# A graph network on one core: products of ones in TensorE's waits at the first ranks and at the head of places 0, 1 and 2

## The chip, the cores and the metric

The kernel runs on one core of a Trainium2 chip. The metric is device time of one execution in microseconds, lower is better. The engines: TensorE (PE: matmuls; PEld: its weight loads), VectorE (DVE), ScalarE (ACT), GpSimd (POOL) and SyncE (SP, which here only issues DMAs). Each runs its own instruction stream in order and waits on semaphores.

## The reference

`x` is 3125 x 256 (fp32), `src` and `dst` hold 50,000 edges, sorted by `dst`. Four layers of a graph network follow on a layer norm:

```python
def sage(x, src, dst, Wl, Wr, b):
    agg = segment_sum(x[src], dst, n)
    deg = segment_sum(ones_like(dst), dst, n)
    return (agg / maximum(deg, 1)[:, None]) @ Wl + x @ Wr + b

h = maximum(layernorm(x), 0)
h = relu(sage(h, ..1)); h = relu(sage(h, ..2)); h = relu(sage(h, ..3))
out = x + sage(h, ..4)
```

## The kernel before

**Counts.** The kernel turns the edge list into a dense matrix `counts` (source node by destination node, fp16, kept in SBUF), so that a layer's sum over edges is a matmul of `H` (the features, split in a high and a low fp16 part) with `counts`. Destinations are cut in 7 chunks of 512 (the last has 53); a chunk at its turn is a *place*, q = 0 to 6, and `ORDER` says which chunk: 5, 6, 4, 3, 2, 1, 0. The counts of a pair of *windows* of 16 destinations in all are made by `step`: VectorE writes one-hot columns for a few edges at a time ("hot" columns, L1460 and L1467), TensorE multiplies them into a PSUM bank (L2091), and ScalarE copies the bank into `counts` (L1817, semaphore `window_stored`).

**Ranks.** Before that, each window's first edge has to be found. The edges lie in 98 rows of 512. `sum_below` (L1969) multiplies 16 times 0/1 comparisons (made by VectorE, L1179, L1182 and, for the low windows, `below_low`, L1230) with a block of ones and so counts edges below each bound: the first rank has 72 columns (into `degree_ps`), the second 108 (`turn_bank`), the third, `rank_low`, 512. ScalarE takes each rank out of PSUM (L1895, semaphore `lo_made`). VectorE then chooses rows (`choose_early`, L1238 and L1250, semaphore `steps_chosen`), and TensorE selects them (`select_rows`, L1978). In between VectorE and ScalarE do the layer norm of chunk after chunk (`h0_moments`, `h0_shift`, `h0_relu`, ...), TensorE its transposes (`h0_turn`, L2036) and the products with `Wr1` (`own_products`, L2048).

**Order of the work.** It is written out by hand, engine by engine: tables such as `between`, `first_round` and `second_round` say what is done after which window or which source tile k. TensorE's stream (from L1966 on): the two first ranks, the two selections, 32 window pairs for place 0 with `select_edges`, `h0_turn`, `own_products` and `rank_low` among them, then `heavy_of(-1)`, then the loop over the places. For each place it adds up 25 source tiles (`add_sources`, L2262; first half "sum", other half "half") while it makes the window pairs of the next place and finishes the place before (`lin_part`, L2156; `narrow_part`, L2205). Degrees come from differences of neighbouring hot cuts (`sum_cuts`, L2297, then `take_degrees` on VectorE, L1541), but in place 1 (`BY_COUNTS`) from the counts themselves (`add_degrees`, L2279: 25 products of two columns, then `degrees` on VectorE, L1605 and L1607). `heavy_of(q)` ends a place's windows: it waits until they are stored, looks in registers for windows with more edges than the planned steps, and branches over them; it does this after place q for q = -1, 0, 1 and on. The beginning of a place on TensorE:

```python
heavy_of(-1)
for q in range(NCH):
    pe.wait_ge(window_stored, filled_after(q - 1))
    if q == BY_COUNTS:
        add_degrees(q)           # waits for own_copied, 2 * IN_LIN
    elif q < NCH - 1:
        sum_cuts(q)              # waits for cuts_made; in place 0 for lo_made, 3
    if q > BY_COUNTS:
        pe.wait_ge(low_done[1], q - 1)
    ...
        if k == 0 and q >= 1:
            pe.wait_ge(agg_scaled[1], 2 * q - 1)
        add_sources(1, q, 0, k, k == 0, k == NT - 1, halves=(0,))
```

The wait on `agg_scaled` is for VectorE's `scale_agg` (L1559), which empties the PSUM bank of the place before. On VectorE's stream the first instruction is a memset of the tail tile of `x` (L1160), for which SP's load of that tile waits; it goes on with the edge rows once their DMA has landed (L1172). After layer 1 come layers 2 to 4, which only sum, multiply and turn; the change touches nothing there.

Of the kernel before, what the change touches and what calls it, by code (L numbers as in the profile page):

```python
# [26 lines left out]
def sage_stack_kernel(nc, x, src, dst, Wl1, Wr1, b1, Wl2, Wr2, b2, Wl3, Wr3, b3, Wl4, Wr4, b4, out):  # L27
# [10 lines left out]
    f32, f16, bf16, i32 = mybir.dt.float32, mybir.dt.float16, mybir.dt.bfloat16, mybir.dt.int32  # L38
    ALU, ACT, AX = mybir.AluOpType, mybir.ActivationFunctionType, mybir.AxisListType

    P = 128
# [6 lines left out]
    CH = TPC * P  # L48
# [37 lines left out]
    for w_, (d0_, _) in enumerate(WINDOWS):  # L86
        PAIR_WINDOWS[d0_ // (2 * WIN)].append(w_)
# [80 lines left out]
    for at_, (w, i) in enumerate(STEP):  # L168
        if i:
            continue  # L170
        k = STEPS[w]
# [8 lines left out]
    BY_COUNTS = 1  # L180
# [75 lines left out]
    def filled_after(q):  # L256

        return sum(len(FILLS[p]) for p in range(-1, q + 1))
# [15 lines left out]
    with ctx:  # L274
        def sb(name, shape, dt):
            return ctx.enter_context(nc.sbuf_tensor(name, shape, dt))

        def pb(name, shape, dt):
            return ctx.enter_context(nc.psum_tensor(name, shape, dt))

        def sem(name):
            return ctx.enter_context(nc.semaphore(name))
# [44 lines left out]
            return at[:, 0:n * P], at[:, n * P:n * (P + KEYS)]  # L327
        WR2 = 2 * 2 * F2
        Wr2_sb = early[:, 0:WR2].bitcast(f32).rearrange("p (k n) -> p k n", k=2)
        cut_at = sb("cut_at", [P, WIN + 2], bf16)  # L330
        minus_one = sb("minus_one", [P, 2], f16)
        plan_all = sb("plan", [P, 2 * NWIN], i32)
# [155 lines left out]
        window_ps = pb("window_ps", [P, 2, 512], f32)  # L488
        degree_ps = pb("degree_ps", [P, 512], f32)
        agg_ps = pb("agg_ps", [P, 2, 512], f32)  # L490
        lin_ps = pb("lin_ps", [P, 2, 512], f32)
        turn_bank = pb("turn_ps", [P, 512], f32)
# [10 lines left out]
        act_order = sem("act_order")  # L503
        pool_order = sem("pool_order")
        pads_set = sem("pads_set")
        consts_made = sem("consts_made")
        dst_loaded = sem("dst_loaded")
        src_loaded = sem("src_loaded")
# [53 lines left out]
        own_copied = sem("own_copied")  # L562
# [130 lines left out]
        IN_LIN = 5  # L693
        FIRST_J = 3
        LAST_DEGREE_TURN_K = 22
        BY_STEPS_IN_AGG = 2
# [442 lines left out]
        def load_heavy(eng, regs, part):  # L1139
            chunks = slice(ORDER[2], NCH) if part == 0 else slice(0, ORDER[2])  # L1140
            eng.wait_ge(plan_made, 3 * part + 3)
            eng.load(regs[1][chunks], heavy[0:1, chunks])
# [13 lines left out]
        def _(dve):  # L1156
            order = Order(dve, dve_order)
            v = nc.vector

            v.memset(x_in[NFULL][:, 0, :], 0.0).then_inc(tail_cleared, 1)  # L1160

            def row_starts(n):
# [804 lines left out]
        def _(pe):  # L1967
            m = nc.tensor.matmul
            def sum_below(below, ps, n, at=0):  # L1969
                for g in range(RG):  # L1970
                    last = m(ps[:, 0:n], ones16[0:RP, :], below[g][:, at:at + n], start=(g == 0), stop=(g == RG - 1))
                last.then_inc(rank_summed, 1)
# [31 lines left out]
            def select_edges():  # L2004
# [6 lines left out]
                                 start=True, stop=True)  # L2011
                last.then_inc(steps_turned, 1)

            pe.wait_ge(consts_made, CONSTS_RANK)
            pe.wait_ge(below_made, 1)
            sum_below([below_high[0:RP, g, :] for g in range(RG)], degree_ps, BOUNDS - CUT)
            pe.wait_ge(below_made, 2)
            sum_below([below_mid[0:RP, g, :] for g in range(RG)], turn_bank, CUT - MID)
            pe.wait_ge(rows_shifted, 2)
            pe.wait_ge(steps_chosen, 1)  # L2020
            select_rows(0, [chosen_first[0:RP, g, :] for g in range(RG)], FIRST)
# [128 lines left out]
            def lin_part(q, j):  # L2150

                n, t = size_of(chunk_at(q))
                if j == 0:
                    pe.wait_ge(agg_scaled[1], 2 * (q + 1))
                h, k = j // 2, j % 2
                last = m(lin_ps[:, h, 0:n], W14[:, 0, k, h * P:(h + 1) * P], aggT[:, k, 0:n], start=(k == 0),  # L2156
                         stop=(k == 1))
                if k == 1:
                    last.then_inc(lin_done[1], 1)
# [110 lines left out]
            def add_degrees(q):  # L2270

                c = chunk_at(q)
                n, t = size_of(c)
                rows_ = P if n == CH else n
                pe.wait_ge(own_copied, 2 * IN_LIN)
                for i in range(t):
                    for k in range(NT):
                        of = slice(0, TAIL if k == NT - 1 else P)
                        last = m(lin_ps[0:rows_, 0, 2 * i:2 * i + 2], counts[of, k, bass.ds((c * TPC + i) * P, rows_)],  # L2279
                                 ones16[of, 0:2], start=(k == 0), stop=(k == NT - 1))  # L2280
                last.then_inc(degree_done, 1)
# [58 lines left out]
            heavy_of(-1)  # L2340
            for q in range(NCH):

                pe.wait_ge(window_stored, filled_after(q - 1))
                if q == BY_COUNTS:
                    add_degrees(q)
                elif q < NCH - 1:
                    sum_cuts(q)
                if q > BY_COUNTS:
                    pe.wait_ge(low_done[1], q - 1)
                for kind, k in script(q):  # L2350
                    if kind == "step":
                        step(*k)
                    if kind == "half":
                        if k == 0 and q >= 1:
                            pe.wait_ge(agg_scaled[1], 2 * q)
                        add_sources(1, q, 0, k, k == 0, k == NT - 1, halves=(1,))
                    if kind == "lin":
                        lin_part(q - 1, k)
                    if kind == "narrow":
                        narrow_part(q - 1, k)  # L2360
                    if kind != "sum":
                        continue
                    if k == 1 and q == BY_COUNTS:
                        pe.wait_ge(degree_inverted, q + 1)
                    if k == CUT_SUM_K and q == NCH - 1:
                        sum_cuts(q)
                    if q == 0 and k in LOW_AT:
                        pe.wait_ge(h0_low, LOW_AT[k])
                    if q == 0 and k in first_round:
                        first_round[k]()  # L2370
                    if q == 1 and k == H0_LATE_K:
                        pe.wait_ge(degrees_taken, 1)
                        pe.wait_ge(norms_made, 3)
                        for j in range(IN_LIN, NCH):
                            h0_turn(j)
                    if q == 1 and k in OWN_LATE_K:
                        own_products(IN_LIN + OWN_LATE_K.index(k))
                    if q == 1 and k == TURN_K:
                        pe.wait_ge(own_copied, 2 * NCH)
                    if k == 0 and q >= 1:  # L2380
                        pe.wait_ge(agg_scaled[1], 2 * q - 1)
                    add_sources(1, q, 0, k, k == 0, k == NT - 1, halves=(0,))
                    if q == BY_COUNTS and k == LAST_DEGREE_TURN_K:
                        turn_degrees(q)
                    if q >= 1 and k == TURN_K:
                        turn(1, q - 1, 0)
                if q == 1:
                    load_heavy(pe, regs, 1)
                    pe.wait_ge(step_tables, 5)
                heavy_of(q)  # L2390
# [100 lines left out]
```

## Time and profile before

| | us |
|---|---|
| median of 3 runs | 659.92 (659.35 to 660.34) |
| the profiled execution, its own time | 660.46 |
| its span, first to last instruction | 658.6 |
| TensorE busy / VectorE / ScalarE / GpSimd | 616.8 / 277.9 / 177.8 / 42.0 |
| mean granted TensorE clock | 0.984 |

The rows below are of one execution; their times count from its first instruction. "Granted clock" is the share of TensorE's full clock (2.4 GHz) that it had in a stretch, 1.00 or 0.50 (1.2 GHz). A row of a timeline merges neighbouring instructions of one group: start, time from the first one's start to the last one's end, engine, line, operands, and how many; in brackets how long the engine stood idle before it and whom it waited for. A matmul's end includes the way through the array, so two rows that follow each other overlap a little. In the chain of waits each line is a piece of the path that ended last; "issue" is time in which nothing that the profile shows was waited for.

### The profile page before, as it was taken

The numbers are of one execution on the slowest core, as the hardware profiler recorded it, in microseconds if no ns is written. First come the engines' busy times: TensorE is split into PE (matmuls) and PEld (weight loads), VectorE is DVE, ScalarE is ACT, GpSimd is POOL, SyncE is SP. The second block draws the span as 40 slices with busy tenths as digits, with TensorE's granted clock in tenths as the row PEclk, the third lists the DMA queues.
The fourth block names the chain that finished last, engine by engine and source line by source line (L and its number), as shares of the span: only waits on it lengthen the run. The fifth ranks groups of instructions, "written<-read, shape, count | busy, mean of one in ns | idle before, by whom it ended". The sixth has DMA issues, their size and how long they took to land.

```text
span 658.6 us, 9693 instructions
## 1 busy us (share of the span) xinstructions
PE 616.8 (94%) x3861; PEld 338.7 (51%) x3862; DVE 277.9 (42%) x529; ACT 177.8 (27%) x379; POOL 42.0 (6%) x93
## 2 busy tenths in 40 slices
PE   5668999798999999998999999999999999999998
PEld 4434565455555445553444445444445555646686
DVE  5979877678888769811212121211120100101011
ACT  3877853364653622300111011121110000000000
POOL 8002100000000000000000000000001011010110
PEclk9977998999999999999999999999999999999999
DMA  8400510520221132241533621344430223032030
GB/s 259 101 0 15 97 33 2 179 56 21 69 34 53 33 53 65 49 136 48 160 88 110 130 81 49 101 119 140 117 121 1 60 65 111 1 111 85 28 112 32
DMA packets 64872, 51.48 MB, mean 78 GB/s; under 512 B 36600, under 2 KB 49437, under 8 KB 64828
## 3 DMA queue, kind: packets, MB, share of 16 engines
q1 hardware_dynamic: 64472, 50.27, 27.3%
q0 software_dynamic: 240, 0.37, 0.7%
q8 instruction: 30, 0.49, 0.4%
q10 hardware_dynamic: 116, 0.24, 0.1%
q14 instruction: 14, 0.11, 0.1%
HBM read 28.68 MB, written 16.60 MB: 69 GB/s over the span
## 4 chain that ended last, share of the span: by engine, by line
PE 78%; DMA 7%; DVE 7%; ACT 3%; issue 2%; SPq 1%; POOL 1%; DVEq 0%; ACTq 0%; POOLq 0%
PE agg_ps L2262 28%; PE window_ps L2262 18%; PE lin_ps L2180 6%; PE lin_ps L2197 5%; PE window_ps L2091 4%; PE lin_ps L2156 3%; DMA rdeg_d<-newH 2%; PE lin_ps L2048 2%; PE window_ps L2238 2%; PE agg_ps L2238 2%; DVE early L1467 1%; DMA rdeg_d<-rdeg 1%; PE lin_ps L2205 1%; ACT counts L1817 1%; DMA newH<-rdeg_d 1%
## 5 line engine op out<-in xcount | busy, mean ns | idle before, releaser
L2262 PE MATMUL agg_ps<-counts,H 128*128 128x512 f16 (+3 forms) x1026 | 235.0, 355 | 2.8 <-DVE aggT L1559 2.5
L2262 PEld LDWEIGHTS agg_ps<-counts,H 128*128 128x128 f16 (+1 forms) x1026 | 79.4, 99 | 58.5 <-issue 12.3
L1817 ACT ACTIVATE counts<-window_ps 128x400 f16<-128x400 f32 x150 | 73.5, 506 | 64.0 <-PE window_ps L2091 50.0
L1460 DVE TENSOR_TENSOR counts<-early 128x2048 f16<-128x2048 bf16 x66 | 77.4, 1214 | 6.2 <-PE window_ps L2091 4.3
L2262 PE MATMUL window_ps<-counts,early 128*128 128x512 f16 (+2 forms) x346 | 77.6, 379 | 0.0
L2262 PE MATMUL window_ps<-counts,H 128*128 128x512 f16 (+2 forms) x291 | 55.3, 346 | 0.0
L2262 PEld LDWEIGHTS window_ps<-counts,early 128*128 128x128 f16 (+1 forms) x346 | 33.6, 98 | 41.5 <-issue 3.4
L1559 DVE SCALAR_TENSOR_TENSOR aggT<-agg_ps,columns,rdeg 128x512 f32<-128x512 f32 (+1 forms) x27 | 17.0, 658 | 80.2 <-PE agg_ps L2262 63.6
L2091 PEld LDWEIGHTS window_ps<-counts 128*128 128x128 f16 x412 | 30.9, 99 | 37.0 <-issue 4.9
L1460 DVE TENSOR_TENSOR early<-early 128x1024 f16<-128x1024 bf16 (+1 forms) x69 | 43.8, 684 | 6.5 <-PE window_ps L2091 4.9
L2262 PE MATMUL agg_ps<-counts,early 128*128 (+4 forms) x297 | 46.5, 314 | 0.0
L2091 PE MATMUL window_ps<-counts 128*128 128x100 f16 x412 | 41.6, 210 | 4.3 <-DVE counts L1460 2.4
L2091 PE MATMUL window_ps<-early 128*128 128x100 f16 (+1 forms) x256 | 32.9, 228 | 9.8 <-DVE early L1467 8.1
L2091 PEld LDWEIGHTS window_ps<-early 128*128 128x128 f16 x256 | 21.3, 101 | 36.6 <-issue 8.1
L2262 PEld LDWEIGHTS window_ps<-counts,H 128*128 128x128 f16 x291 | 24.9, 98 | 29.2 <-issue 1.5
L1122 POOL TENSOR_TENSOR newH<-newH,plan 128x256 f32<-128x256 f32 (+1 forms) x25 | 17.3, 723 | 345.0 <-DMA newH<-in_x_dram 345.0
L1862 ACT ACTIVATE newT<-newT,columns 128x512 f32<-128x512 f32 (+1 forms) x21 | 13.4, 663 | 91.4 <-DVE newT L1695 65.8
L1559 DVE SCALAR_TENSOR_TENSOR aggT<-window_ps,columns,rdeg 128x512 f32<-128x512 f32 (+1 forms) x13 | 9.0, 712 | 67.1 <-PE window_ps L2262 64.3
L1580 DVE SCALAR_TENSOR_TENSOR partsT<-newT,columns,partsT 128x512 f16<-128x512 f32 (+1 forms) x16 | 10.6, 662 | 57.7 <-ACT partsT L1876 57.6
L2262 PEld LDWEIGHTS agg_ps<-counts,early 128*128 128x128 f16 (+1 forms) x297 | 22.0, 97 | 24.3 <-issue 1.1
L1681 DVE TENSOR_TENSOR newT<-lin_ps,newH 128x512 f32<-128x512 f32 (+1 forms) x11 | 7.3, 666 | 50.6 <-PE lin_ps L2180 50.6
L1862 ACT ACTIVATE newT<-lin_ps,columns 128x512 f32<-128x512 f32 (+1 forms) x14 | 8.9, 633 | 69.2 <-PE lin_ps L2197 69.2
(246 smaller groups left out, 636.3 us busy)
## 6 DMA issues: line engine op xcount, KB each, us to landing
selfT<-hT_d SPq DMA_DIRECT2D x18, 512.0 KB, 4.1
rdeg<-rdeg_d SPq DMA_DIRECT2D x24, 256.0 KB, 4.5
hT_d<-newT SPq DMA_DIRECT2D x12, 512.0 KB, 4.4
counts<-in_x_dram SPq DMA_DIRECT2D x6, 512.0 KB, 8.0
hT_d<-counts SPq DMA_DIRECT2D x6, 512.0 KB, 3.4
newH<-in_x_dram SPq DMA_DIRECT2D x6, 512.0 KB
out_dram<-newT SPq DMA_DIRECT2D x5, 512.0 KB
hT_d<-newT SPq DMA_DIRECT2D x6, 256.0 KB, 3.8
```

Source lines behind the costliest of these rows:

```text
L1122: nc.gpsimd.tensor_tensor(x4[0:q, i, :], x4[0:q, i, :], b4rows[0:q, :], ALU.add).then_inc(x4_biased, 1)
L1460: v.tensor_tensor(hots_of(group).rearrange("p r a (n d) -> p r a n d", d=2), pairs.unsqueeze(1).unsqueeze(1).broadcast_to([P, n, 2, P // 2 ...
L1559: v.scalar_tensor_tensor(out=aggT[:, h, 0:n], in0=(agg_ps, window_ps)[bank][:, h, 0:n], scalar=unscale[:, l - 1:l], in1=rdeg[:, 0:n], op0= ...
L1817: a.activation(counts[:, :, 2 * w * WIN:2 * (w + 1) * WIN].rearrange("p t (a w) -> p a t w", a=2), window_bank(FILL_AT[w])[:, 0:2 * KEYS]. ...
L1862: a.activation(newT[:, h, 0:n], source, ACT.Relu, bias=bT[:, bias + h:bias + h + 1]).then_inc(relu_done[l], 1)
L2048: last = m(h0_ps(j)[h][:, 0:n], W14[:, 1, k, h * P:(h + 1) * P], x_T[c][:, k, 0:n], start=(k == 0), stop=(k == 1))
L2091: m(window_bank(at)[:, key0:key0 + keys], one_src, one_key, start=(j == 0), stop=(j == STEPS[w] - 1)).then_inc(hot_used, 1)
L2156: last = m(lin_ps[:, h, 0:n], W14[:, 0, k, h * P:(h + 1) * P], aggT[:, k, 0:n], start=(k == 0), stop=(k == 1))
L2180: last = m(lin_ps[0:rows_, g, i * D:(i + 1) * D], h, w, start=(j == 0), stop=(j == len(ops) - 1))
L2197: last = m(lin_ps[:, h, 0:n], w, r, start=(i == 0), stop=(i == len(ops) - 1))
L2238: last = m((agg_ps, window_ps)[bank][:, h, cols], tile[:, part, h * P:(h + 1) * P], counts[0:rows_, k, c * CH + g * HALF_CH:c * CH + (g + ...
L2262: last = m((agg_ps, window_ps)[bank][:, h, 0:n], tile[:, part, h * P:(h + 1) * P], counts[0:rows_, k, chunk_cols(c, n)], start=first and p ...
```

## The change

Twenty-five products are added to TensorE's stream by a new helper, `keep_clock(ps, times)`. Each multiplies one column of ones, repeated to 128 x 128, with the same column repeated to 128 x 512, and writes a PSUM bank that holds nothing wanted at that moment; the next use of the bank overwrites it, and nobody reads the products. The ones are a new tile of two columns, set by a memset that is now VectorE's first instruction. There are eleven products at the very start, before the wait for the first rank's input; two between the second rank and the first selection; four at the head of place 0; four at the head of place 1, after a wait on `own_copied` that `add_degrees` had, and has, too; four in place 2 before the wait on `agg_scaled`.

```diff
@@ -327,6 +327,7 @@
             return at[:, 0:n * P], at[:, n * P:n * (P + KEYS)]
         WR2 = 2 * 2 * F2
         Wr2_sb = early[:, 0:WR2].bitcast(f32).rearrange("p (k n) -> p k n", k=2)
+        one = sb("one", [P, 2], f16)
         cut_at = sb("cut_at", [P, WIN + 2], bf16)
         minus_one = sb("minus_one", [P, 2], f16)
         plan_all = sb("plan", [P, 2 * NWIN], i32)
@@ -503,6 +504,7 @@
         act_order = sem("act_order")
         pool_order = sem("pool_order")
         pads_set = sem("pads_set")
+        one_set = sem("one_set")
         consts_made = sem("consts_made")
         dst_loaded = sem("dst_loaded")
         src_loaded = sem("src_loaded")
@@ -1157,6 +1159,7 @@
             order = Order(dve, dve_order)
             v = nc.vector

+            v.memset(one[:, :], 1.0).then_inc(one_set, 1)
             v.memset(x_in[NFULL][:, 0, :], 0.0).then_inc(tail_cleared, 1)

             def row_starts(n):
@@ -2011,11 +2014,19 @@
                                  start=True, stop=True)
                 last.then_inc(steps_turned, 1)

+            def keep_clock(ps, times):
+
+                for _ in range(times):
+                    m(ps, one[:, 0:1].broadcast_to([P, P]), one[:, 0:1].broadcast_to([P, CH]), start=True, stop=True)
+
+            pe.wait_ge(one_set, 1)
+            keep_clock(window_ps[:, 0, :], 11)
             pe.wait_ge(consts_made, CONSTS_RANK)
             pe.wait_ge(below_made, 1)
             sum_below([below_high[0:RP, g, :] for g in range(RG)], degree_ps, BOUNDS - CUT)
             pe.wait_ge(below_made, 2)
             sum_below([below_mid[0:RP, g, :] for g in range(RG)], turn_bank, CUT - MID)
+            keep_clock(window_ps[:, 0, :], 2)
             pe.wait_ge(rows_shifted, 2)
             pe.wait_ge(steps_chosen, 1)
             select_rows(0, [chosen_first[0:RP, g, :] for g in range(RG)], FIRST)
@@ -2340,6 +2351,11 @@
             heavy_of(-1)
             for q in range(NCH):

+                if q == 0:
+                    keep_clock(turn_bank[:, :], 4)
+                if q == BY_COUNTS:
+                    pe.wait_ge(own_copied, 2 * IN_LIN)
+                    keep_clock(lin_ps[:, 0, :], 4)
                 pe.wait_ge(window_stored, filled_after(q - 1))
                 if q == BY_COUNTS:
                     add_degrees(q)
@@ -2377,6 +2393,8 @@
                         own_products(IN_LIN + OWN_LATE_K.index(k))
                     if q == 1 and k == TURN_K:
                         pe.wait_ge(own_copied, 2 * NCH)
+                    if k == 0 and q == BY_STEPS_IN_AGG:
+                        keep_clock(lin_ps[:, 0, :], 4)
                     if k == 0 and q >= 1:
                         pe.wait_ge(agg_scaled[1], 2 * q - 1)
                     add_sources(1, q, 0, k, k == 0, k == NT - 1, halves=(0,))
```

## Rows read from the trace of the kernel before

**Rows 1.** Page of the kernel before: engine totals, and granted clock in 40 slices
```profile
PE 616.8 (94%) x3861; PEld 338.7 (51%) x3862; DVE 277.9 (42%) x529; ACT 177.8 (27%) x379; POOL 42.0 (6%) x93
...
PEclk9977998999999999999999999999999999999999
```

**Rows 2.** Stretches: from:to, length, busy us (instructions) by engine, clock, DMA, GB/s
```profile
27.42:37.66 10.24, 7.17 (x36) 3.42 (x35) 9.93 (x31) 9.31 (x23) 0.00 (x0) 1.00 0.03 7
37.66:44.49 6.83, 4.91 (x16) 2.23 (x17) 6.52 (x29) 6.61 (x22) 0.00 (x0) 0.50 0.00 1
44.49:51.32 6.83, 4.37 (x29) 2.55 (x27) 3.05 (x14) 4.26 (x14) 0.00 (x0) 1.00 0.01 4
51.32:58.14 6.82, 5.02 (x20) 2.21 (x19) 6.43 (x25) 4.01 (x13) 0.00 (x0) 0.50 0.07 9
...
105.93:109.34 3.41, 3.41 (x21) 3.35 (x21) 2.55 (x8) 1.18 (x4) 0.00 (x0) 0.50 0.03 6
...
129.82:133.24 3.42, 3.42 (x21) 1.82 (x19) 1.69 (x2) 1.51 (x3) 0.00 (x0) 0.50 0.37 112
```

**Rows 3.** Timeline of TensorE, 5 to 16: start, length, line, operands, count [idle before]
```profile
6.32 1.12 PE L1971 MATMUL degree_ps<-counts,newH 98*128 98x72 f16 x16 [6.32 <-POOL early L1038]
7.29 1.62 PE L1971 MATMUL turn_ps<-counts,newH 98*128 98x108 f16 x16
9.01 1.86 PE L1978 MATMUL agg_ps<-counts 98*128 98x64 f16 x32
10.97 3.28 PE L1978 MATMUL lin_ps<-counts 98*128 98x115 f16 x32
```

**Rows 4.** Timeline of VectorE, 4.9 to 11
```profile
5.00 0.30 DVE L1172 TENSOR_SCALAR counts<-H 98x32 f16<-98x32 int32 x1 [3.86 <-DMA H<-in_dst_dram]
...
6.09 1.14 DVE L1182 TENSOR_TENSOR counts<-counts 98x1728 f16<-98x1728 f16 x1
7.83 0.31 DVE L1238 TENSOR_TENSOR counts<-counts 98x64 f16<-98x64 f16 x1 [0.59 <-ACT counts L1895]
...
9.34 0.16 DVE L1238 TENSOR_TENSOR counts<-counts 98x7 f16<-98x7 f16 x1 [0.48 <-issue]
```

**Rows 5.** Timeline of all engines from the start: ScalarE takes the two ranks
```profile
7.47 0.32 ACT L1895 ACTIVATE counts<-degree_ps,counts 128x72 f16<-128x72 f32 x1 [0.91 <-PE degree_ps L1971]
...
8.95 0.35 ACT L1895 ACTIVATE counts<-turn_ps,counts 128x108 f16<-128x108 f32 x1 [1.15 <-PE turn_ps L1971]
```

**Rows 6.** Timeline of TensorE, 40.5 to 47: the rank of the low windows
```profile
41.02 5.32 PE L1971 MATMUL degree_ps<-counts,newH 98*128 98x512 f16 x16 [1.31 <-DVE counts L1230]
```

**Rows 7.** Chain that ended last, 44 to 56: start, length, what
```profile
47.54 1.98 ACT counts L1817 x5
49.52 0.58 ACT counts L1895
```

**Rows 8.** Timeline of TensorE, 47 to 54: where place 0 begins
```profile
50.50 0.40 PE L2297 MATMUL degree_ps<-aggT,newH 128*128 128x512 f16 x1 [2.17 <-ACT counts L1895]
```

**Rows 9.** Chain that ended last, 100 to 110: where place 1 begins
```profile
103.70 0.61 issue
104.31 0.94 PE lin_ps L2279 x25
...
105.75 1.84 PE window_ps L2036 x8
```

**Rows 10.** Timeline of TensorE, 126 to 140: where place 2 begins
```profile
129.12 0.59 PE L2262 MATMUL agg_ps<-counts,H 128*128 128x512 f16 x2 [1.73 <-DVE aggT L1559]
...
130.81 1.05 PE L2262 MATMUL agg_ps<-counts,H 128*128 128x512 f16 x2
...
131.99 1.05 PE L2262 MATMUL agg_ps<-counts,H 128*128 128x512 f16 x2
...
135.28 0.59 PE L2262 MATMUL agg_ps<-counts,H 128*128 128x512 f16 x2
...
135.89 0.59 PE L2262 MATMUL agg_ps<-counts,H 128*128 128x512 f16 x2
```

## The prediction

> **What bounds the kernel now.** I began with the page's shares and its slices [rows 1]: TensorE is busy for 616.8 us, 94% of the span, so an edit pays only where TensorE runs slowly or where another engine waits for it. The clock line is below 9 in three slices only, all in the first fifth. The second view cuts the span where the granted clock changes [rows 2]. It is at 0.50, the 1.2 GHz level, in four stretches: 37.66 to 44.49, 51.32 to 58.14, 105.93 to 109.34 and 129.82 to 133.24; the reader is to see TensorE busy all the time in the last two (3.41 of 3.41, 3.42 of 3.42), while in the second VectorE is just as full (6.43 of 6.82). Third, TensorE's timeline at the start [rows 3]. The profile shows a clock of 1.00 there, but the durations say otherwise: 16 products of 72 columns in 1.12 us and 32 of 115 columns in 3.28 us are some 1.2 columns a nanosecond, the lower level. So the ranks run at half rate too, though no row of the clock says it.
>
> Who waits for those ranks is in VectorE's timeline [rows 4] and in ScalarE's two rows [rows 5]: TensorE sums a rank, ScalarE takes it out of PSUM (0.32 and 0.35), VectorE chooses rows with it. VectorE stands still for 0.59 before 7.83 and 0.48 before 9.34. Last come the chains of waits where places 0 and 1 begin [rows 7, 9] and TensorE's timeline where places 0 and 2 begin [rows 8, 10].
>
> **The change part by part.** Price of one product of 512 columns: the rank of the low windows has 16 of them in 5.32 us from 41.02 [rows 6]; the first 3.47 us of that lie before 44.49, at half rate. 3.47/(2b) + 1.85/b = 16 gives b = 0.22 at full rate and 0.45 at half. No row has a product whose two operands are both one repeated column. Below, 0.22 stands; above, 0.45, as if it always went at half rate. I take 0.22, since every other 512-column product goes at what the clock gives.
>
> *The memset of ones* lies in VectorE's idle 3.86 us before 5.00 [rows 4]: nothing. The memset behind it, for which SP's load of the tail of x waits, comes later by less than that memset's own length; nothing again.
>
> *Eleven products before the first rank.* TensorE does nothing until 6.32 [rows 3]. They start at about 1.0 and at half rate take 11 x 0.45 = 4.9, so they end by 5.9 and delay nothing. If they lift the clock, the second rank, which starts at 7.29 when its input is made (6.09 + 1.14 [rows 4]), is shorter: 16 x 108 columns go from about 1.6 to 0.9. VectorE's second choice moves from 9.34 to 8.64, 0.70 earlier; the first, which the end of 6.09 + 1.14 also holds, moves by 0.44 and no longer decides. From there VectorE is nearly full until 41 (9.93 of 10.24 from 27.42 on [rows 2]), so the 0.70 arrives at the low rank. There half is lost: if the clock still rises at 44.49, that rank only starts 0.70 earlier into the low stretch, and 0.70 at half rate is worth 0.35. I take -0.35; bounds 0 (no lift) and -0.70.
>
> A reason to doubt the lift: TensorE is busy almost without a pause from 6.32 to 14.25 [rows 3], and the clock stays low. The difference that I see is in size: stretches that ended with a rise held 512-column products [rows 6, 10] or fp32 transposes [rows 9], while those before 14.25 have 64 to 115 columns. The eleven have 512, so I take the lift. The Trainium skill, page "TensorE: Matmul & The Clock Gate", section "What's actually happening", says that the clock is throttled by default and that activity releases it. The trace agrees at 44.49, and disagrees from 6.32 to 14.25. By that rule the start gains what I took, and by the row nothing; the sum is then 658.1 or 658.5.
>
> *Two products between the second rank and the selection.* 0.44 at full rate, 0.9 at half. The selection waits for VectorE's first choice anyway, and its result is wanted only once VectorE is through the second choice and the first statistics, past 12: nothing. At half rate too the cover is over 1 us.
>
> *Four products at place 0.* They stand behind heavy_of(-1), which waits for the last window store (1.98 from 47.54, so 49.52 [rows 7]). So they do not fill the wait of 2.17 us [rows 8]; they follow most of it. In place 1 TensorE takes 0.61 from the store to its first product [rows 9]; taken here, it arrives at 50.13. Four products end at 51.0, and the sum of cuts, now at 50.50 [rows 8], just after the low rank's row is taken (49.52 + 0.58), starts 0.5 later. Queued behind it: take_degrees on VectorE, then bases_late and the hot columns for which TensorE waits next. All on the path: +0.5; bounds 0 (it arrives earlier) and +1.4 (at half rate). If the low stretch 51.32 to 58.14 vanishes, TensorE saves half of 5.02, but VectorE has 6.43 of 6.82 to do there [rows 2], so 0.4 at most comes through. I take nothing, since the long idle before the products stays.
>
> *Four products at place 1*, again behind the wait and the branch of heavy_of(0): from 104.31 on, so they push the 25 degree products of two columns by 0.9, and with them VectorE's inverse and the transposes at 105.75 [rows 9]: +0.9; bounds 0 and +1.8. The wait on own_copied that moves ahead of them was met when ScalarE copied place 4's own products, long before; nothing. What they may give: between the last window product and 105.75 there are now almost only two-column products. With 2048 columns in the middle the fall at 105.93 should stay away. The 3.41 us at half rate are full of transposes, worth 1.7: net -0.8.
>
> *Four products at place 2* stand before the wait on agg_scaled. TensorE sits idle there for 1.73 us until 129.12 [rows 10]; four take 0.9, at half rate 1.8: hidden, or 0.1 over. The fall at 129.82 should go. In the low stretch a step of the loop takes 1.18 (130.81 to 131.99), later 0.61 (135.28 to 135.89); VectorE is busy for 1.69 of 3.42 [rows 2] and can keep up. Worth 3.42/2 = 1.7: -1.7; bounds 0 and -1.7. What is late next is VectorE's hot columns, which then run level with TensorE.
>
> SP and POOL issue nothing more; chains of DMAs that begin at these places start earlier by as much as TensorE does.
>
> The sum: -0.35 + 0.5 - 0.8 - 1.7 = -2.35. The profiled execution took 660.46 (its span is 658.6), so 658.1. The median of the runs shown is 0.54 lower; I don't take that off, since those runs may have had one low stretch fewer, and what isn't there can't be won. A measurement of this kernel tells about 0.2%, 1.3 us, from no change; 658.1 is 1.8 under the median.
>
> **The rivals.** *Place 1 keeps its fall.* For: the products come after the wait for the store, not in it, and the two-column products remain. Against: the four split the quiet stretch. Then +0.9 stands alone: -0.35 + 0.5 + 0.9 - 1.7 = -0.65, 659.8: no change.
>
> *Slower: the clock falls before the products*, in the waits ahead of places 0 and 1, so that they run at half rate on the path: +1.4 and +1.8, both low stretches still there. -0.35 + 1.4 + 1.8 - 1.7 = +1.15, 661.6. It decides if the clock falls before 50.1 and before 104.3; in the trace it fell at 51.32 and 105.93, which speaks against it.
>
> *The products don't count*: constant operands don't hold the clock, as the ranks didn't raise it. All stretches stay, the delays of 0.5 and 0.9 too: 661.9. Against: the rank at 41.02 has ones as weights and raised it.
>
> *More than I count*: the clock stays up through the ranks to 27.4 and at the low rank. The 0.70 is then kept whole, and 3.47 us at half rate there save 1.7: 2.05 more, 656.0. For: every start shifts, so falls can shift too. Against: nothing is added between 14 and 41.
>
> **How the numbers follow.** Forecast 48%, place 1 keeps its fall 20%, slower 10%, don't count 8%, more 14%. Predicted: 658.1. The forecast's own spread, with one or two terms at a bound, is 656.8 to 659.2. The range goes from 656.2, which leaves out about half of the last rival (7%), to 661.2, which leaves out two thirds of the two slow ones (12%; a third of them may fall short of it): 19% is outside. Faster by over 0.2% (below 658.6): 41 of the 48 and the 14, 55%. Slower (above 661.2): the 12. The rest, 33%, within.
>
> **What would show it.** Ranks: 16 products of 108 columns in about 0.9, VectorE's second choice at about 8.6. Place 0: sum of cuts 0.5 later than its ScalarE row would let it. Place 1: four products ahead of the degrees, no 0.50 stretch over the transposes, eight of them in 1.1 in place of 1.84. Place 2: idle before the first sum about 0.8, no low stretch. It would be wrong if the low stretches are still there in the clock, or have moved elsewhere; or if the first rank is at its old length.

## The result, and the profile after

The changed kernel takes 656.51 us (median of 4 runs, 655.7 to 658.08), the kernel before 660.0 beside it (4 runs): a ratio of 0.9947 [0.993, 0.9963], so 2.4 to 4.6 us faster. Forecast were 658.1 and a range of 656.2 to 661.2: the side and the range hold, and the gain is about twice the 1.8 that I had forecast against the median. The profiled execution is the slowest of the four, 658.08 with a span of 656.3, which is 2.35 under the span of the profile before (to the hundredth, from the two traces). My terms summed to -2.35 as well. That agreement is luck: the terms of the ranks and of place 1 missed, and stretches that I had not priced made up for them.

The page of the changed kernel, totals and clock line; they answer to [rows 1]:

```profile
PE 618.9 (94%) x3886; PEld 336.8 (51%) x3887; DVE 278.5 (42%) x530; ACT 178.2 (27%) x379; POOL 41.1 (6%) x93
...
PEclk9678998999999999999999999999999999999999
```

TensorE has 25 products more and is busy 2.1 us longer, in a shorter span. Stretches of the changed kernel at the places where the granted clock changes (columns as in [rows 2]):

```profile
4.50:14.74 10.24, 5.51 (x102) 4.21 (x99) 8.97 (x30) 3.56 (x6) 10.01 (x37) 1.00 0.89 286
...
38.63:45.46 6.83, 5.15 (x14) 1.82 (x14) 5.59 (x26) 5.20 (x17) 0.00 (x0) 0.50 0.01 2
...
55.70:59.11 3.41, 3.08 (x14) 1.28 (x13) 3.26 (x16) 2.28 (x8) 0.00 (x0) 0.50 0.09 5
106.90:110.31 3.41, 3.14 (x15) 3.14 (x16) 2.50 (x8) 1.13 (x3) 0.00 (x0) 0.50 0.01 2
128.00:133.24 5.24, 4.33 (x36) 2.31 (x35) 4.78 (x6) 1.81 (x4) 0.53 (x1) 1.00 0.39 102
```

Against [rows 2]: the stretch around the low rank is as long as before and ends 0.97 later; the one behind place 0 is half as long; the one over place 1's transposes is still there; the one at place 2 is gone. A low stretch that [rows 2] doesn't have lasts from 14.74 to 28.39. TensorE's timeline at the start, answering to [rows 3]:

```profile
0.93 4.29 PE L2020 MATMUL window_ps<-one 128*128 128x512 f16 x11 [0.93 <-DVE one L1162]
5.92 0.68 PE L1974 MATMUL degree_ps<-counts,newH 98*128 98x72 f16 x16 [0.70 <-POOL early L1040]
6.89 0.93 PE L1974 MATMUL turn_ps<-counts,newH 98*128 98x108 f16 x16 [0.29 <-DVE counts L1185]
7.67 0.60 PE L2020 MATMUL window_ps<-one 128*128 128x512 f16 x2
8.10 1.10 PE L1981 MATMUL agg_ps<-counts 98*128 98x64 f16 x32
9.89 1.80 PE L1981 MATMUL lin_ps<-counts 98*128 98x115 f16 x32 [0.69 <-DVE counts L1253]
```

The ranks went from 1.12 and 1.62 to 0.68 and 0.93, the selections from 1.86 and 3.28 to 1.10 and 1.80: the higher level. VectorE's timeline there, answering to [rows 4]:

```profile
4.63 0.28 DVE L1175 TENSOR_SCALAR counts<-H 98x32 f16<-98x32 int32 x1 [3.45 <-DMA H<-in_dst_dram]
...
8.26 0.16 DVE L1241 TENSOR_TENSOR counts<-counts 98x7 f16<-98x7 f16 x1 [0.32 <-POOL counts L1040]
```

The second choice comes 1.08 earlier; 0.37 of it is an edge row that landed earlier (4.63 against 5.00), the other 0.71 the ranks'. TensorE's timeline at place 0 (answering to [rows 8]), then at place 1, then at place 2 ([rows 10]):

```profile
50.30 1.04 PE L2020 MATMUL turn_ps<-one 128*128 128x512 f16 x4 [1.84 <-ACT counts L1820]
51.18 0.40 PE L2308 MATMUL degree_ps<-aggT,newH 128*128 128x512 f16 x1
...
104.75 1.03 PE L2020 MATMUL lin_ps<-one 128*128 128x512 f16 x4 [1.16 <-ACT counts L1820]
105.71 0.95 PE L2290 MATMUL lin_ps<-newH,counts 128*53 128x2 f16 x25
...
107.17 1.97 PE L2047 MATMUL window_ps<-newH,counts 128*128 128x128 f32 x8 [0.30 <-DVE newH L1610]
...
128.35 1.03 PE L2020 MATMUL lin_ps<-one 128*128 128x512 f16 x4
130.30 0.61 PE L2273 MATMUL agg_ps<-counts,H 128*128 128x512 f16 x2 [0.91 <-DVE aggT L1562]
...
130.92 0.59 PE L2273 MATMUL agg_ps<-counts,H 128*128 128x512 f16 x2
131.52 0.59 PE L2273 MATMUL agg_ps<-counts,H 128*128 128x512 f16 x2
```

At places 0 and 1 the four stand behind the idle time and push what follows; at place 2 they stand in it, and a step of the loop (130.92 to 131.52) takes 0.60 where it took 1.18.

**Where every profile gains and loses.** The table cuts each profile of this study at the same VectorE instructions (heads: where these start in the profile before). An entry is the length of that stretch less its length in the profile before, worked out from VectorE's timelines; the last two columns are the span's difference and the times after 100 at which the granted clock fell to 0.50. Left out are 9.3 to 31.6 (0 to +0.41), what lies past 164.5, and a fall that most profiles have in the last us of the span or behind it.

```
              5.0-  31.6- 47.3- 51.2- 62.5-  105.4- 128.7- 134.6-
              9.3   47.3  51.2  62.5  105.4  128.7  134.6  164.5   span   falls after 100
before_again  -0.09 +0.31 +0.00 +0.16 +0.02  +0.00  +0.00  +0.69  +2.70  106, 130, 291
before_third  +0.06 +0.19 +0.01 +0.09 +0.01  +0.00  +0.00  -0.31  +1.09  106, 130
place0_only   -0.11 +0.39 +0.68 +0.00 -0.09  -0.02  +0.00  -0.02  +1.15  106, 130
place1_only   -0.06 +0.94 +0.00 +0.47 +0.99  -0.16  +0.00  +0.34  +2.64  108, 132
place2_only   +0.14 +1.46 +0.00 +0.42 -0.01  +0.00  -1.74  -0.26  +2.80  108, 313
ranks_only    -0.49 +0.66 -0.12 +0.38 +0.06  +0.00  -1.66  -0.73  -2.14  107
ranks_later   -0.44 +0.45 +0.00 +0.22 +0.00  -0.01  -1.66  +2.30  +0.78  106, 154
after         -0.71 +0.82 +0.55 -0.24 +0.99  -0.15  -1.74  -1.21  -2.35  107
after_again   -0.78 +1.58 +0.55 -0.45 +0.36  -1.65  -1.74  -0.61  -2.38  none
zeros         -0.69 +0.23 +0.54 -0.45 +1.00  -0.35  -1.74  -0.38  -1.27  106
without_place1 -0.51 +1.82 +0.55 -0.44 -0.62 -1.65  -1.74  -0.50  -3.48  none
in_the_waits  -0.86 +0.83 -0.13 +0.47 +0.00  -1.65  -1.74  -0.48  -2.93  none
waits_no_place1 -0.81 +0.75 -0.12 +0.43 +0.07 +0.07 -1.74 -0.42  -0.98  107, 288
```

### The profile page after: what moved, and what is told of

It reads as the page before. It is cut to its first block, busy times and chain, and to the rows that moved or that the text cites. A ratio compares the mean times of both kernels' runs of the same rounds, so it can differ in the third digit from the quotient of the medians.

```text
span 656.3 us, 9743 instructions
## 1 busy us (share of the span) xinstructions
PE 618.9 (94%) x3886; PEld 336.8 (51%) x3887; DVE 278.5 (42%) x530; ACT 178.2 (27%) x379; POOL 41.1 (6%) x93
## 4 chain that ended last, share of the span: by engine, by line
PE 79%; DVE 7%; DMA 6%; ACT 3%; issue 2%; SPq 1%; POOL 1%; DVEq 0%; POOLq 0%; ACTq 0%
PE agg_ps L2273 28%; PE window_ps L2273 19%; PE lin_ps L2191 6%; PE lin_ps L2208 5%; PE window_ps L2102 4%; PE lin_ps L2167 3%; DMA rdeg_d<-newH 2%; PE lin_ps L2059 2%; PE window_ps L2249 2%; DVE early L1470 2%; PE agg_ps L2249 2%; DMA rdeg_d<-rdeg 1%; DMA newH<-rdeg_d 1%; PE lin_ps L2216 1%; SPq L898 1%
## 5 line engine op out<-in xcount | busy, mean ns | idle before, releaser
L1820 ACT ACTIVATE counts<-window_ps 128x400 f16<-128x400 f32 x150 | 73.7, 506 | 61.6 <-PE window_ps L2102 47.3
```

Of the source, the lines that this page charges most:

```text
L1820: a.activation(counts[:, :, 2 * w * WIN:2 * (w + 1) * WIN].rearrange("p t (a w) -> p a t w", a=2), window_bank(FILL_AT[w])[:, 0:2 * KEYS]. ...
```

## The experiments

They ran in three groups, each with its own runs of the kernel before: 662.98 (34 runs), 664.16 (18) and 663.31 (11). Only ratios within a group are compared; "under" and "over" in us are the ratio's distance from 1 times that median.

### Each piece alone (first group)

ranks_only keeps of the change the two calls at the ranks, the other three keep one place each:

```
 ranks_only                                place0_only
+keep_clock(window_ps[:, 0, :], 11)       +if q == 0:
 ...                                      +    keep_clock(turn_bank[:, :], 4)
+keep_clock(window_ps[:, 0, :], 2)
 place1_only                               place2_only
+if q == BY_COUNTS:                       +if k == 0 and q == BY_STEPS_IN_AGG:
+    pe.wait_ge(own_copied, 2 * IN_LIN)   +    keep_clock(lin_ps[:, 0, :], 4)
+    keep_clock(lin_ps[:, 0, :], 4)
```

**ranks_only.** Expected:

> Only the eleven and the two products at the ranks. Theory (the gain is made where place 2 begins, the ranks give little): VectorE's second choice comes 0.7 us earlier after the edge rows have landed, but the low rank takes part of it back, so the time is 0.2 to 0.7 under before. Rival (the ranks carry most of the 3.5 us, because an earlier start also moves the later falls of the clock): 2 us or more under before.

Measured: 659.32 (11 runs), 0.9942 [0.9924, 0.9959], 3.8 under: my theory falls, the rival stands. The trace shows 0.49 at the ranks, for 0.7 foreseen, and the largest piece where nothing was added: the fall near 130 is missing. The stretch 128.70 to 134.60, each from its own profile's start, of the kernel before, of its third profile and of ranks_only, in this order, one fence for each:

```profile
128.70:134.60 5.90, 5.48 (x37) 3.44 (x38) 2.84 (x6) 2.52 (x5) 0.52 (x1) 0.71 0.25 73
```
```profile
128.70:134.60 5.90, 5.16 (x35) 3.11 (x35) 3.13 (x5) 2.28 (x5) 0.52 (x1) 0.71 0.25 72
```
```profile
128.70:134.60 5.90, 4.78 (x45) 3.27 (x46) 4.37 (x8) 2.52 (x5) 0.53 (x1) 1.00 0.30 81
```

The clock is at 1.00 throughout, TensorE gets through 45 products in 4.78 us instead of 37 in 5.48 (or 35 in 5.16), and its idle time before the first (1.86, from 127.95) is no shorter than the 1.73 of [rows 10].

**place0_only.** Expected:

> Only the four products at the head of place 0. Theory: the sum of cuts starts 0.5 us later; the low stretch behind it is halved, which gives 0.3 to 0.5 back since VectorE is full there; time between 0.1 under and 0.5 over before. Rival (the products pay for themselves, because TensorE was the bound in that stretch): 1 us or more under before.

Measured: 661.75 (12 runs), 0.9983 [0.996, 1.0007]; the interval holds both cases. The trace has the delay (+0.68 at 47.3 to 51.2) and a low stretch from 51.72 to 58.54 as before.

**place1_only.** Expected:

> Only the four products at the head of place 1, behind the wait for the stored windows. Theory: the degree products start 0.9 us later and the clock still falls over the transposes, so 0.9 us over before. Rival (they hold the clock in most executions, the profile of the changed kernel was an exception): 0.8 us under before, and no stretch at 0.50 near 106.

Measured: 663.76 (12 runs), 1.0021 [1.0004, 1.0039], 1.4 over (0.3 to 2.6): the theory's side. Its delay is +0.99, its fall is still there at 107.84. Four products behind the wait, their price on the path, nothing back.

**place2_only.** Expected:

> Only the four products in place 2. Theory: the low stretch after 130 goes at no cost, 1.7 us under before. Rival (VectorE's hot columns are the next bound there): 0.5 us under before or less, TensorE waits for VectorE between 130 and 140. A gain of 2.5 or more would say that the stretch after it gains too.

Measured: 661.92 (12 runs), 0.9983 [0.9965, 1.0002], 1.1 under, which decides between neither. The trace does what I forecast at the place itself (-1.74, no fall near 130), but has a fall at 313 that no other profile has:

```profile
313.07:316.49 3.42, 3.42 (x5) 1.33 (x4) 0.69 (x1) 0.59 (x1) 0.00 (x0) 0.50 0.33 95
```

TensorE is full in it, after 2.35 of idle time up to 312.18, and the stretch between 309.7 and 327.2 is 1.70 longer for it.

### The whole again, and moved or cut (second group)

**after_again** is the changed kernel once more. Expected:

> The changed kernel once more, for its median on this chip and a second profile. Theory (the eleven products fix when the clock first rises, and with it where it can fall later): first rise again 3.6 us after the first product, near 4.5, falls again near 14.7, 38.6 and 106.9, none near 130; time 3.5 us under before, with a spread of 2 or 3 us. Rival (each execution falls elsewhere): rises and falls differ from the first profile by up to 3 us, and the spread of the times is as wide as before's 6 us.

Measured: 660.81 (10 runs), 0.9953 [0.9934, 0.9972], 3.1 under, as the first time (0.9947). The trace is another: the clock rises at 5.44, falls at 15.68, rises at 32.74, falls at 39.57, rises at 46.40 and then stays. The same stretch that [rows 2] shows at 0.50:

```profile
105.93:109.34 3.41, 3.11 (x52) 2.95 (x50) 2.31 (x8) 1.00 (x2) 0.00 (x0) 1.00 0.04 6
```

One program, two executions, one with the fall at place 1 and one without: whether this fall comes differs between executions, and one profile of each kernel can't price it. Against the first profile this one wins 1.50 there and loses 0.76 at the low rank, where its rise came 0.94 later still. So the theory falls: the first product came at 0.93 and 0.94 in the two profiles, and the rises and falls behind it differ. The times spread over 4.1 us (658.05 to 662.1), between the 2 or 3 of the theory and the 6 of the rival.

**ranks_later** moves the products at the ranks behind the wait for the constants, eight of them:

```
-keep_clock(window_ps[:, 0, :], 11)
 pe.wait_ge(consts_made, CONSTS_RANK)
+keep_clock(window_ps[:, 0, :], 8)
```

and has none at the places. Expected:

> Ranks alone, but eight products in place of eleven, behind the wait for the constants, so they start near 2.8 in place of 0.9. Theory (the first product fixes the later rises and falls): the first rise comes 3.6 us after them, near 6.4, and every later rise and fall is 1.9 us later than in ranks_only as well (falls near 16.7, 40.6, 108.9), so other stretches are hit and the time differs from ranks_only by 1 us or more. Rival (the rises and falls have nothing to do with the products): the falls come at the same times as in ranks_only, or anywhere, and the time is that of ranks_only within 0.5 us.

Measured: 660.93 (9 runs), 0.9951 [0.9928, 0.9974], 3.3 under. They start at 2.92, the clock rises at 7.18, between the two ranks: 1.10 for the first, 0.93 for the second. The gain in the runs does not hang on the first rank. The theory falls here too: the falls at 14.01, 37.90 and 106.17 are 0.8 earlier than those of ranks_only (14.81, 38.71, 106.97), not 1.9 later. The ratio is 0.0009, or 0.6 us, from that of ranks_only, which was run in another group, so the times settle nothing between theory and rival. The profile again lacks the fall near 130 and has one at 153.95 instead (+2.30).

**without_place1** leaves place 1's three lines out of the change. Expected:

> The change without the four products of place 1. Theory (they cost 0.9 us and hold nothing): 0.9 us faster than the changed kernel. Rival (together with the other products they do hold the clock in most executions): 0.5 us or more slower than the changed kernel.

Measured: 657.47 (6 runs), 0.9909 [0.988, 0.9939], 6.0 under the kernel before, 2.9 under the changed kernel beside it. TensorE's timeline at place 1:

```profile
105.35 0.93 PE L2290 MATMUL lin_ps<-newH,counts 128*53 128x2 f16 x25 [1.16 <-ACT counts L1820]
106.21 0.28 PE L2273 MATMUL agg_ps<-counts,H 128*128 128x53 f16 x4
106.79 1.09 PE L2047 MATMUL window_ps<-newH,counts 128*128 128x128 f32 x8 [0.30 <-DVE newH L1610]
```

The degrees follow the wait at once, and eight transposes take 1.09 with no product ahead of them: in this execution the clock stayed up there without place 1's products. The runs are on the theory's side, at three times its 0.9; of that the trace shows the 0.98 that the products cost (below).

**in_the_waits** keeps all, but places 0 and 1 issue their products ahead of the wait for the store:

```
+keep_clock(turn_bank[:, :], 4)
 heavy_of(-1)
 ...
+if q == 0:
+    pe.wait_ge(own_copied, 2 * IN_LIN)
+    keep_clock(lin_ps[:, 0, :], 4)
 heavy_of(q)
```

Expected:

> The four products of place 0 and of place 1 moved ahead of the wait for the stored windows and the branch, into TensorE's idle time. Theory: they delay nothing, 0.5 us and 0.9 us earlier than in the changed kernel, so 1.4 us faster than it; whether the falls go I expect for place 1 in half of the executions. Rival (the delay is not on the path, or the idle time left behind the products lets the clock fall more often): within 0.5 us of the changed kernel or slower.

Measured: 657.85 (5 runs), 0.9906 [0.9876, 0.9936], 6.2 under the kernel before and 3.1 under the changed kernel beside it: the theory's side, at over twice its 1.4. TensorE's timeline at place 0, then place 1:

```profile
48.42 1.03 PE L2020 MATMUL turn_ps<-one 128*128 128x512 f16 x4
50.63 0.40 PE L2308 MATMUL degree_ps<-aggT,newH 128*128 128x512 f16 x1 [1.17 <-ACT counts L1898]
...
103.59 1.03 PE L2020 MATMUL lin_ps<-one 128*128 128x512 f16 x4
104.91 0.93 PE L2290 MATMUL lin_ps<-newH,counts 128*53 128x2 f16 x25 [0.28 <-issue]
```

In the wait they cost nothing: -0.13 at 47.3 to 51.2 in place of +0.55, and +0.00 at place 1 in place of +0.99. But the stretch behind place 0 is 0.47 longer than in the profile before, where the changed kernel has it 0.24 and 0.45 shorter; the rest of the 3.1 I can't point to.

### The kernel before again, zeros, and both mendings (third group)

**before_again** and **before_third** are the kernel before. Expected:

> The kernel before once more, for a second profile of it. Theory: its one profile, 660.46, is among the better executions, and a usual one (663 to 664 in the two earlier groups of runs) has more time at 1.2 GHz; then this profile shows a stretch of 0.50 in the clock that the first has not, or one that ends later, each worth about 1.7 us per 3.4 us where TensorE is full. Rival: the lows lie as in the first profile (falls near 38, 51, 106 and 130) and the time is still over 662; then the loss is not in the clock, and the segments between VectorE's markers say where it is.

> A third profile of the kernel before. If executions draw their rises and falls anew each time, its falls differ from both other profiles in at least one place; if the times of the falls belong to the program, they are those of the first profile within 1 us. In both cases the second choice of VectorE starts at 9.2 to 9.5 and the ranks take about 1.1 and 1.6, since nothing precedes them on TensorE.

Measured: 663.15 and 661.54, one run each. The falls near 38, 52, 106 and 130 come in both; the first also falls at 290.90, which the theory had said, but that is no more than 1.05 (277.6 to 309.7) of its 2.70. 0.69 is a longer wait near 153, the rest is spread. The third profile's four falls (38.06, 51.72, 106.33, 130.22) come 0.40 behind the first's, so by what I had set for it they belong to the program; the one fall that an execution adds in these three profiles is that at 290.90. The profile on which I predicted is the best of three.

**zeros** writes 0.0 in place of 1.0. Expected:

> The changed kernel with products of zeros in place of ones; the time of a product is the same. If only the running of products counts for the clock: the first rise at 4.5 to 6.1, ranks of about 0.7 and 0.9, and 6 to 3 us under the kernel before, as the changed kernel in the second group of runs (-3.1). If what the operands hold counts (zeros switch nothing): ranks of 1.1 and 1.6, the first rise after 27, and the delays at places 0 and 1 (0.5 and 0.9) without what the ranks give, so 0 to 1.5 over the kernel before.

Measured: 658.74 (6 runs), 0.9939 [0.9917, 0.9962], 4.0 under. By the runs, products of zeros do the same. The rise is recorded at 6.87, past the 4.5 to 6.1 that I had set for it and past all six profiles with eleven products of ones (4.50 to 6.07), and the first rank straddles it; whether zeros raise the clock later one profile can't tell:

```profile
0.93 4.88 PE L2020 MATMUL window_ps<-one 128*128 128x512 f16 x11 [0.93 <-DVE one L1162]
6.32 0.92 PE L1974 MATMUL degree_ps<-counts,newH 98*128 98x72 f16 x16 [0.51 <-POOL early L1040]
7.29 0.94 PE L1974 MATMUL turn_ps<-counts,newH 98*128 98x108 f16 x16
```

**waits_no_place1** has place 0's products ahead of heavy_of(-1), as in_the_waits, and none at place 1, as without_place1. Expected:

> The changed kernel with place 0's four products ahead of heavy_of(-1) and its wait, and without place 1's four. Theory: each product that stands behind its wait costs its own length on the path (0.55 at place 0, 0.95 at place 1) and gives nothing there that it would not give in the wait; then this is 1.5 under the changed kernel, with a ratio to the kernel before of 0.990 to 0.993, level with the two kernels that mend one of the two places (0.9909, 0.9906) or up to 0.5 under them. Rival: place 0's products pay for themselves by what they do to the stretch behind them only when they come right before the sum of cuts; then it is 0.3 to 1 slower than the one without place 1's.

Measured: 659.18 (6 runs), 0.9939 [0.9918, 0.9959], 4.0 under. The two mendings do not add up: the ratio is outside the 0.990 to 0.993 of the theory, though its interval reaches into it, and it is the ratio of zeros, which mends nothing. The table shows why moving place 0 alone is worth little. The stretch 51.2 to 62.5 is 0.24 to 0.45 shorter in the four profiles that have the ranks' products and place 0's right before the sum of cuts, and 0.43 and 0.47 longer in the two that have them in the wait: there, the low stretch behind place 0 (52.55 to 59.38) is as long as in the kernel before. So 0.7 to 0.9 comes back at the head, for the 0.68 (0.55 + 0.13) that it costs. That is the rival's mechanism, though not its size: by the ratios, from two groups, this version is 2.0 slower than the one without place 1's, for 0.3 to 1 foreseen. This profile also falls at 107 and 288.

## Why the prediction was right, and where it was wrong

The number came out right, but not by my account: in the runs the ranks' products alone (3.8 and 3.3 under) give as much as the whole change (3.5 and 3.1), and I had given them 0.35.

**The ranks: the lift right, the way of its gain wrong; the step that failed.** The clock rose before the ranks, and VectorE's second choice came 0.71 earlier for 0.70 forecast. I let that arrive at the low rank because VectorE "is nearly full until 41", but the row for it begins at 27.42, and 0.39 was lost before 17.1: two VectorE instructions of 0.20 and 0.19 (L1276, L1277) took 0.66 and 0.58. By 47.3 the rest is gone too, since the rise at the low rank came late (+0.82). How much of that the change did I can't say: in that stretch the profile before is the shortest of the fourteen, and its two other profiles have +0.31 and +0.19. What the traces show of the gain lies far behind the ranks. First, the fall near 130: it is in all five profiles that have neither the ranks' products nor place 2's, and in neither of the two that have the ranks' alone (-1.66). These two have 1.5 falls after 100 on average, the five 2.2; at some 1.7 us each that is 1.2 us. Second, past 327.2 all eight profiles with the ranks' products are 0.71 to 0.75 shorter than the profile before, the six without them -0.47 to +0.17, on average -0.06: 0.7 more. There SP issues a pair of transposing DMAs, ScalarE's and VectorE's parts for the next place wait for it, and TensorE for them. Timelines of SP, ScalarE and TensorE of the kernel before, then of SP and ScalarE of the changed kernel, which has no wait of TensorE there:

```profile
334.43 3.27 SPq L896 DMA_TRANSPOSE H<-partsT  x2
...
339.01 0.34 ACT L1876 ACTIVATE partsT<-newT,columns 128x53 f16<-128x53 f32 x1 [1.85 <-DMA H<-partsT]
...
339.71 0.27 PE L2227 MATMUL turn_ps<-ident,partsT 128*117 128x128 f16 x1 [0.68 <-DVE partsT L1580]
```
```profile
332.81 2.53 SPq L898 DMA_TRANSPOSE H<-partsT  x2
...
336.65 0.34 ACT L1879 ACTIVATE partsT<-newT,columns 128x53 f16<-128x53 f32 x1 [1.12 <-DMA H<-partsT]
```

That pair takes 2.53 or 2.54 in the eight, 2.80 to 3.44 in the six. So some 1.9 of the 3.3 to 3.8 are accounted for, from single executions; the 0.5 at the start of ranks_only and ranks_later is no longer there by 47.3. My prediction let products act only where they stand, and that is what failed. Why products before 8.7 go with a fall that is missing near 130 and with a shorter issue near 334 is open, and no run here tests it; nor does one part the two products behind the second rank from those ahead of the first, as all eight versions have both. Between 105.4 and 128.7 ranks_only does the same work in the same time as the kernel before.

**Place 0: delay right (0.55 for 0.5), "I take nothing" for the stretch behind it wrong.** The low stretch there became half as long, and 0.24 came back. In after_again and without_place1 it was gone, and 1.06 to 1.08 came back by place 1 (-0.45 and -0.44 up to 62.5; up to 105.4 another 0.63 and 0.62, in after_again ahead of place 1's 0.99). That is over my ceiling of 0.4, which counted only what VectorE does inside the low stretch. With TensorE slow, VectorE waits for it behind the stretch as well; its wait in the kernel before, then in after_again:

```profile
68.76 0.69 DVE L1460 TENSOR_TENSOR early<-early 128x1024 f16<-128x1024 bf16 x1 [1.39 <-PE window_ps L2091]
```
```profile
69.25 0.69 DVE L1463 TENSOR_TENSOR early<-early 128x1024 f16<-128x1024 bf16 x1 [0.66 <-PE window_ps L2102]
```

By itself, without the ranks' products, place 0 left the low stretch as long as before and gave nothing back (+0.00).

**Place 1: price right (0.99 for 0.9), return wrong.** I forecast -1.7 from a fall that would stay away; the fall came, as the rival with 20% had it. Whether it comes isn't settled by these products: with them right before the degrees it came three times (after, place1_only, zeros) and was missing once (after_again); with them ahead of the wait it was missing (in_the_waits); without them it was missing once (without_place1) and came in all the others. What the traces settle is the price: between after_again and without_place1, neither of which falls after 50, the stretch before 105.4 differs by 0.98.

**Place 2: right at the place, but not a gain of its own.** -1.74 for -1.7, and an idle time of 0.91 for 0.8. Alone it measured 1.1 under, with an interval that holds both nothing and the whole. But both profiles with the ranks' products alone have -1.66 there with nothing added at place 2, so beside them place 2's products are worth no more than 0.08 in these traces. My sum gave the whole -1.7 to place 2.

**The other rivals.** The clock did not fall before the products at place 0 or 1 (four in 1.04 and 1.03). That the products don't count falls with the rise at 4.50. That the clock stays up through the ranks to 27.4 did not happen either: it fell at 14.74.

**The sum.** Terms on record: -0.35 + 0.5 - 0.8 - 1.7. In the profile: the ranks nothing by 47.3 (-0.37 - 0.71 + 0.39 + 0.82 = +0.13), place 0 +0.55 - 0.24, place 1 +0.99 - 0.15, place 2 -1.74; that is -0.46. The other 1.89 of the 2.35 came after 134.6 (-1.21 up to 164.5, then +0.77, -0.44 and -0.27 up to 309.7, and -0.73 past 327.2), and none of that was in my sum. The first of these is in good part a shorter wait of TensorE, in the kernel before and in the changed kernel:

```profile
154.42 0.31 PE L2091 MATMUL window_ps<-counts 128*128 128x100 f16 x3 [1.66 <-ACT counts L1817]
```
```profile
152.13 0.31 PE L2102 MATMUL window_ps<-counts 128*128 128x100 f16 x3 [0.60 <-ACT counts L1820]
```

The Trainium skill, page "TensorE: Matmul & The Clock Gate", section "What's actually happening", says that activity releases the throttle, and that the point at which the clock first rises varies from run to run of one kernel. The traces agree with both: the rise at 4.50 behind products from 0.93 on, and the rise at 5.44 in the second profile of the same kernel. I had used the first statement and not the second. That the falls vary too is in the traces: at 106.90 in the one, none there in the other; it speaks against pricing a low stretch by one profile.

## What to carry to other kernels

A product that nobody reads is free only ahead of a wait; behind it, it costs its own length on the path (four of 512 columns: 0.88 from the first start to the next work), so put it before the wait instruction, or leave it out where the trace shows no return. What it gives can hang on where it stands, though: moved into the wait, place 0's cost nothing and no longer shortened the low stretch behind them. Before a low stretch of the clock is entered into a sum at its full price, take a second and third profile of the same kernel, and let medians decide: a fall can be in one execution and not in the next, and what an edit does to it need not happen where the edit stands. Price each piece beside the others, not only alone: two pieces can remove the same fall. Of the versions here the change without place 1's products, or with the products of both places in their waits, has the best ratios: 0.9909 and 0.9906 against 0.9953 for the changed kernel beside them. The intervals still touch, and waits_no_place1, with place 0's in the wait and none at place 1, came out at 0.9939, so the lead isn't sure.

## What the runs showed of the hardware that I had not expected

- A fall of the clock can come where TensorE is full and nothing of the program has changed: at 290.90 in one of three profiles of the kernel before, 0.1 us after a run of products of 512 columns began. The stretch in before_again:

```profile
290.90:294.31 3.41, 3.41 (x10) 1.21 (x8) 0.69 (x1) 0.00 (x0) 0.00 (x0) 0.50 1.02 284
```

  Before it the engine worked on pairs of products of 4 to 180 columns, without a pause from 287.61 to 290.79; the changed kernel has the same pairs up to 287.32 and no fall there.
- Products of zeros lift the clock too (rise at 6.87, ranks of 0.92 and 0.94; 0.9939 in the runs).
- The mean granted clock of an execution is no measure of its speed. The runs of the kernel before show 0.982 to 0.987, those of ranks_only 0.971 to 0.977, and ranks_only is the faster; at 0.984 alone, runs of the kernel before take 660.64 to 663.73 (first group). Ahead of the first recorded rise the trace has 1.00, though the rate is half [rows 3]; the early rise of the changed kernel makes the low stretch from 14.74 to 28.39 visible, while VectorE's work between 17.1 and 31.6 takes the same time in both, within 0.02.
